# Convolution slots issued in pairs, eight PSUM banks by table, and x1 kept for two images

## The reference

```python
# layer 0: 32 small models of 16 channels, grouped 3x3 neighbourhood, residual
perception = concat([x] + 8 shifted copies, axis=1)      # 9*512 channels
per_g = perception.reshape(b, 32, 144, h, w)
hdn = relu(einsum('bmchw,mdc->bmdhw', per_g, w1) + b1)   # 64 hidden per model
x = x + einsum('bmdhw,mcd->bmchw', hdn, w2) + b2
# layer 1: non-local attention over the 1024 pixels, 128 inner channels
theta, phi, g = (w @ x + b for each of the three)        # 512 -> 128
attn = softmax(theta^T phi); y = attn g                  # 1024 x 1024
out = batchnorm(w_w @ y + w_b) + x
```

## Time and profile before

| | |
|---|---|
| median of 3 runs | 1491.43 us (1491.01 to 1491.73) |
| profiled execution, its own time | 1491.56 us |
| its span, first to last instruction | 1489.8 us |
| TensorE (PE) busy | 1466.9 us, 98% |
| VectorE (DVE) busy | 832.0 us, 56% |
| ScalarE (ACT) busy | 749.4 us, 50% |
| GpSimd (POOL) busy | 241.8 us, 16% |
| DMA | 144 GB/s over the span, 41.4% of 16 engines |
| granted TensorE clock, mean | 1.000 |

### The profile page before, as it was taken

How to read it: one execution, slowest core, us unless ns; L and a number is a source line. 1 busy time by engine, 2 the same in 40 slices (tenths; PEclk the granted TensorE clock), 3 DMA queues, 4 the chain that set the end, 5 groups by cost and what they waited for, 6 DMA issues and landing times.

```text
span 1489.8 us, 27659 instructions
## 1 busy us (share of the span) xinstructions
PE 1466.9 (98%) x10364; PEld 772.7 (52%) x10364; DVE 832.0 (56%) x1033; ACT 749.4 (50%) x1175; POOL 241.8 (16%) x134
## 2 busy tenths in 40 slices
PE   7999999999999999999999999999999999999998
PEld 1454636446464464644546455463644636446467
DVE  1374654746546564565646547465474654656456
ACT  3464463645545454455544646446363554645444
POOL 0040210403103030130401204021040210303003
PEclk9999999999999999999999999999999999999999
DMA  4153452535425263261633625346253452535301
GB/s 134 48 185 117 167 202 90 197 113 173 170 90 208 102 209 135 104 232 67 214 127 128 225 81 196 113 160 211 90 196 114 164 179 90 199 110 200 144 29 57
DMA packets 129280, 214.84 MB, mean 144 GB/s; under 512 B 7280, under 2 KB 78448, under 8 KB 129264
## 3 DMA queue, kind: packets, MB, share of 16 engines
q1 hardware_dynamic: 129264, 214.62, 41.4%
HBM read 110.25 MB, written 104.33 MB: 144 GB/s over the span
## 4 chain that ended last, share of the span: by engine, by line
PE 87%; DVE 4%; issue 3%; DMA 3%; ACT 2%; SPq 0%; ACTq 0%
PE ps L400 27%; PE ps L427 8%; PE ps L414 8%; PE ps L441 6%; PE ps L442 6%; PE ps L443 6%; PE ps L471 4%; PE ps L473 4%; PE ps L472 4%; DMA rows_out<-probs 3%; PE ps L487 3%; DVE neg_max L838 2%; PE ps L457 2%; PE ps L459 2%; PE ps L458 2%
## 5 line engine op out<-in xcount | busy, mean ns | idle before, releaser
L400 PE MATMUL ps<-windows,w_main 64*64 64x512 f32 x4096 | 476.1, 598 | 12.1 <-DMA w_left<-in_w_lefts 9.3
L657 ACT ACTIVATE hidden<-ps,columns 128x512 f32<-128x512 f32 x512 | 310.1, 690 | 265.9 <-PE ps L414 265.9
L1042 POOL TENSOR_TENSOR probs<-probs,row_inv 128x1024 f32<-128x1024 f32 x128 | 241.1, 1893 | 1231.7 <-DVE row_inv L844 1231.7
L400 PEld LDWEIGHTS ps<-windows,w_main 64*64 64x64 f32 x4096 | 142.1, 132 | 303.3 <-issue 302.3
L858 DVE TENSOR_TENSOR x_lo<-x_lo,x_hi 128x1024 fp32r<-128x1024 f32 x120 | 153.7, 1301 | 108.2 <-ACT x_hi L692 107.1
L685 ACT ACTIVATE probs<-ps,neg_max 128x1024 f32<-128x1024 f32 x128 | 143.9, 1124 | 126.4 <-DVE neg_max L838 123.4
L838 DVE TENSOR_REDUCE neg_max<-ps 128x1 f32<-128x1024 f32 x128 | 155.7, 1217 | 14.3 <-PE ps L459 10.6
L441 PE MATMUL ps<-x_hi,wp_hi 128*128 128x512 f32 x384 | 153.5, 400 | 0.6 <-issue 0.6
L442 PE MATMUL ps<-x_lo,wp_hi 128*128 128x512 f32 x384 | 150.0, 391 | 0.0
L443 PE MATMUL ps<-x_hi,wp_lo 128*128 128x512 f32 x384 | 149.6, 390 | 0.0
L849 DVE STREAM_TRANSPOSE probs<-probs 128x1024 f32<-128x1024 f32 x120 | 144.6, 1224 | 0.0
(11 more groups left out here) (78 smaller groups left out, 1511.7 us busy)
## 6 DMA issues: line engine op xcount, KB each, us to landing
rows_out<-probs SPq DMA_DIRECT2D x120, 512.0 KB, 2.8
x_lo<-rows_out SPq DMA_DIRECT2D x120, 512.0 KB, 5.5
out<-out_half SPq DMA_DIRECT2D x30, 1024.0 KB, 4.2
windows<-in_x SPq DMA_DIRECT2D x64, 298.0 KB, 4.1
windows<-in_x SPq DMA_DIRECT2D x64, 264.0 KB, 5.3
rows_out<-g_t SPq DMA_DIRECT2D x15, 512.0 KB, 2.6
g_raw<-rows_out SPq DMA_DIRECT2D x15, 512.0 KB, 7.3
out<-x SPq DMA_DIRECT2D x8, 256.0 KB, 2.1
```

The costliest lines, as they stand in the source:

```text
L400: product = mm(ps[HIDDEN * which:HIDDEN * (which + 1), hidden_bank(n, s, q), :], w_main[rows, p, which, :], shifted(windows[rows, chunk % ...
L657: activation(hidden[:, s % HIDDEN_HELD, q, :], ps[:, hidden_bank(n, s, q), :], ACT.Relu, bias=b1s[:, column:column + 1]).then_inc(hidden_r ...
L1042: nc.gpsimd.tensor_tensor(rows, rows, row_inv[:, e].to_broadcast([P, PIXELS]), ALU.mult).then_inc(normalized, 1)
```

## The change

It leaves the arithmetic and the number of matmuls as they are. `batch(n)` issues two slots in a row (both `mains`, then both `left`), then one piece of attention, then both `dx`; the eight banks are given out by tables; x1 has a buffer for each of two images, and `out` is added in place there, so that `out_half` goes. `hidden` is held for two slots. Because a buffer is now chosen by the parity of n, the loop body is two images and runs 7 turns, with the first image's batch in front of it. The wait at the end of TensorE's body (`out_added`) and that of VectorE's (`stored`) go. `w_left` is loaded in four pieces. All of the engines' orders change, also in the epilogue.

```diff
-HIDDEN_HELD = 4
+HIDDEN_HELD = 2
-        x1 = sb("x1", [P, BLOCKS, PIXELS])
+        x1s = sb("x1s", [P, 2, BLOCKS, PIXELS])
-        out_half = sb("out_half", [P, BLOCKS, HALF])
+        SLOT_BANKS = [(6, 7, 4, 5), (0, 1, 2, 3), (4, 5, 0, 1), (2, 3, 6, 7),
+                      (2, 3, 6, 7), (1, 4, 5, 0), (5, 0, 2, 3), (6, 7, 1, 4)]
+        FIRST_IMAGE_BANKS = [(4, 5, 6, 7), (0, 1, 2, 3)]
+        DX_BANKS = [6, 7, 5, 0, 1, 4, 0, 2]
+        ROW_BANKS = [0, 2, 0, 2, 6, 4, 0, 2]
+        Y_BANKS = [4, 5]
+        Z_BANKS = [(2, 3, 6, 7), (3, 6, 7, 1)]
...
+                elif s == 1:
+                    await_exp(n - 1, 2 + q // 2)
+                elif s == 2:
+                    await_exp(n - 1, 5 + q // 2)
...
+                elif s == 5 and q == 1:
+                    await_ahead(y_split, (n - 1) * 2 + 1)
...
             def scores(n, i):
+                if i >= HALF_QBLOCKS and not last_image(n):
+                    pe.wait_ge(hidden_ready, (n + 1) * SLOT_PAIRS + 2 * (i - HALF_QBLOCKS + 1))
...
             def batch(n, parity):          # TensorE, the order after
                 project(n, 0, TH)
                 project(n, 0, PH)
                 project(n, 1, PH)
                 project(n, 0, G)
                 scores(n, 0)
                 scores(n, 1)
                 project(n, 1, TH)
                 scores(n, 2)
                 project(n, 1, G)
                 scores(n, 3)
                 mains(n + 1, 0)
                 mains(n + 1, 1)
                 left(n + 1, 0)
                 left(n + 1, 1)
                 for i in range(HALF_QBLOCKS, QBLOCKS):
                     scores(n, i)
                 dx(n + 1, 0)
                 dx(n + 1, 1)
                 mains(n + 1, 2)
                 mains(n + 1, 3)
                 left(n + 1, 2)
                 left(n + 1, 3)
                 attend(n, 0)
                 dx(n + 1, 2)
                 dx(n + 1, 3)
                 mains(n + 1, 4)
                 mains(n + 1, 5)
                 left(n + 1, 4)
                 left(n + 1, 5)
                 output(n, 0)
                 dx(n + 1, 4)
                 dx(n + 1, 5)
                 mains(n + 1, 6)
                 mains(n + 1, 7)
                 left(n + 1, 6)
                 left(n + 1, 7)
                 attend(n, 1)
                 dx(n + 1, 6)
                 dx(n + 1, 7)
                 output(n, 1)
-            with pe.Fori(0, BATCH - 1) as n:
-                batch(n)
+            batch(0, 0)
+            with pe.Fori(0, BATCH // 2 - 1) as i:
+                batch(i * 2 + 1, 1)
+                batch(i * 2 + 2, 0)
```

More of the change, by code:

```diff
@@ L184, in conv_attention @@
         w_main_loaded = [sem(f"w_main_loaded_{g}") for g in range(GROUPS)]
-        w_left_loaded = sem("w_left_loaded")
+        w_left_loaded = [sem(f"w_left_loaded_{g}") for g in range(GROUPS)]
         w2_loaded = sem("w2_loaded")
@@ L315, in batch @@
                 fetch_row(n, 7)
[L316 to L317 removed]
+                store_half(n, parity, 0)
+                store_half(n, parity, 1)
             def load_w_main(grp):
@@ L325, in _ @@
                 load_top(0, b)
-            sp.dma_start(w_left[:, :, :, :], w_lefts).then_inc(w_left_loaded, 16)
+            load_w_left(0)
             sp.dma_start(columns[:, :], per_channel).then_inc(columns_loaded, 16)
[L328 to L331, removed]
+            for grp in range(1, GROUPS):
+                load_w_main(grp)
+                load_w_left(grp)
+                if grp == 1:
+                    sp.dma_start(w2s[:, :, :], w2_pairs).then_inc(w2_loaded, 16)
             for b in range(BLOCKS):
@@ L409, in left @@
                 half, grp = divmod(s, GROUPS)
+                if first_image(n) and half == 0:
+                    await_ahead(w_left_loaded[grp], 16)
                 for q in range(GROUP_PAIRS):
@@ L455, in scores @@
                 for half in range(2):
-                    bank, cols = ps[:, 2 * (i % 2) + half, :], slice(half * HALF, (half + 1) * HALF)
+                    bank, cols = ps[:, score_bank(n, i) + half, :], slice(half * HALF, (half + 1) * HALF)
                     mm(bank, tp_hi[:, TH, rows], tp_hi[:, PH, cols], start=True, stop=False)
@@ L475, in attend, with output @@
                 last.then_inc(y_summed, 1)
-            def output(n, h, k):
-                if k == 0:
+            def output(n, h):
+                pe.wait_ge(y_rounded, n * 2 + h + 1)
+                for k in range(BLOCKS):
                     if h == 0:
[L480 to L491, removed]
@@ L493, in batch @@
-            def batch(n):
+                        pe.wait_ge(hidden_ready, (n + 1) * SLOT_PAIRS + 4 * GROUP_PAIRS + k + 1)
+                    bank, c = ps[:, Z_BANKS[h][k], :], slice(k * P, (k + 1) * P)
+                    mm(bank, ww_hi[:, c], y_hi[:, :], start=True, stop=False)
+                    mm(bank, ww_lo[:, c], y_hi[:, :], start=False, stop=False)
+                    if k == 0:
+                        pe.wait_ge(y_split, n * 2 + h + 1)
+                    mm(bank, ww_hi[:, c], y_lo[:, :], start=False, stop=True).then_inc(z_summed, 1)
@@ L506, in batch @@
                 mains(n + 1, 0)
-                scores(n, 4)
-                scores(n, 5)
+                mains(n + 1, 1)
                 left(n + 1, 0)
-                scores(n, 6)
-                scores(n, 7)
-                mains(n + 1, 1)
                 left(n + 1, 1)
-                mains(n + 1, 2)
-                left(n + 1, 2)
+                for i in range(HALF_QBLOCKS, QBLOCKS):
+                    scores(n, i)
                 dx(n + 1, 0)
                 dx(n + 1, 1)
+                mains(n + 1, 2)
@@ L518, in batch @@
                 mains(n + 1, 3)
+                left(n + 1, 2)
                 left(n + 1, 3)
                 attend(n, 0)
[L521 to L528, removed]
                 dx(n + 1, 2)
                 dx(n + 1, 3)
-                mains(n + 1, 6)
-                attend(n, 1)
@@ L533, in batch @@
-                left(n + 1, 6)
-                output(n, 1, 0)
-                output(n, 1, 1)
+                mains(n + 1, 4)
+                mains(n + 1, 5)
+                left(n + 1, 4)
+                left(n + 1, 5)
+                output(n, 0)
                 dx(n + 1, 4)
                 dx(n + 1, 5)
-                output(n, 1, 2)
-                output(n, 1, 3)
+                mains(n + 1, 6)
                 mains(n + 1, 7)
+                left(n + 1, 6)
                 left(n + 1, 7)
-                pe.wait_ge(out_added, n * SLOTS + SLOTS)
+                attend(n, 1)
@@ L545, in transpose_ww @@
+                dx(n + 1, 6)
+                dx(n + 1, 7)
+                output(n, 1)
             def transpose_ww():
@@ L768, in _ @@
             nc.scalar.preload_act_table(ACT.Exp)
-            relus(0, 0)
-            for s in range(1, SLOTS - 1):
+            for s in range(SLOTS):
                 relus(0, s)
-                round_x1(0, s - 1)
-                if s == SLOTS - 3:
+                if 2 <= s < 2 + GROUPS:
+                    round_x1(0, 0, s - 2)
+                if s == SLOTS - 2:
                     act.wait_ge(w_l1_loaded, 16 * W_L1_DMAS)
@@ L947, in batch @@
                 split_row(n, 7)
-                sum_x1(n + 1, 2)
                 split_y(n, 1)
-                sum_x1(n + 1, 3)
-                for k in range(BLOCKS):
-                    add_out(n, 1, k)
-                sum_x1(n + 1, 4)
-                for s in range(GROUPS):
-                    split_x1(n + 1, s)
-                sum_x1(n + 1, 5)
-                split_x1(n + 1, 4)
-                split_x1(n + 1, 5)
-                dve.wait_ge(stored, (n + 1) * 32)
+                split_x1(n + 1, 1 - parity, 0)
+                split_x1(n + 1, 1 - parity, 1)
+                split_x1(n + 1, 1 - parity, 2)
+                split_x1(n + 1, 1 - parity, 3)
+                add_out(n, parity, 1, 0)
+                sum_x1(n + 1, 1 - parity, 6)
+                add_out(n, parity, 1, 1)
+                add_out(n, parity, 1, 2)
+                add_out(n, parity, 1, 3)
+                sum_x1(n + 1, 1 - parity, 7)
             steps = [0]
@@ L981, in _ @@
             chain(tt(shift[:, :], shift[:, :], bn[:, BETA, :], ALU.add))
-            for s in range(SLOTS - 2):
-                sum_x1(0, s)
-                split_x1(0, s)
-                if s == SLOTS - 4:
+            for s in range(SLOTS):
+                sum_x1(0, 0, s)
+                if 2 <= s < 2 + GROUPS:
+                    split_x1(0, 0, s - 2)
+                if s == SLOTS - 2:
                     dve.wait_ge(w_l1_loaded, 16 * W_L1_DMAS)
```

361 lines of the change are left out of this document (198 added, 163 removed).

## The result

The changed kernel takes 1479.37 us (1478.04 to 1480.44, 4 runs) against 1491.58 us for the kernel before on the same chip: a ratio of 0.9918, 95% interval 0.9901 to 0.9935, so faster, by 12.2 us. The forecast was 1469 us in a range of 1457 to 1484: the direction and the range held, the gain was a little over half of the one forecast. The profiled execution took 1478.04 us with a span of 1476.2.

The account below looks back on a forecast made before the run. TensorE's own stream bounds the kernel, busy 90.90 of 91.14 us per turn. Span: 1489.8 - 28.3 (loop) + 0.3 (prologue) + 0.1 (epilogue) + 6 (code fetches) = 1467.9 us; forecast 1469 us, range 1457 to 1484.

Parts of the forecast that it names:

- Fewer changes of shape: TensorE's stream: 17 stretches of one shape per turn instead of 30, saving 2.2 us of 91.14.
- The waits of the old order go: TensorE's waits for the exponential and the late bank of the sixth mains vanish, 0.5 us per turn.
- The x1 chain: VectorE's splits and sums ahead of project(n, 1, PH): 10.3 us against 10.2, a wait of about 0.1 us, no reserve.
- Scores 4 and the relus: scores(4) writes banks that relus 0 and 1 read, so TensorE waits 0.5 us behind the two left.
- Turned rows: Row 3's split ends about 1 us ahead of the first attend, row 7 has 3 us; cost 0, at most 1.
- The longer body: The doubled loop body may not fit on chip; fetches at six jumps back cost 1 us each, 6 us.
- Prologue +0.3, epilogue +0.1: Code outside the loop: prologue gains and losses sum to +0.3 us, epilogue's to +0.1, give or take 3.
- The softmax: Exponentials of rows 3 and 6 finish shortly before mains(1) and mains(2) want their banks; taken as 0, at most 0.5 each.
- `dx` 5: TensorE's dx 5 waits 0.15 us for its relus.
- waits take the gain back: Rival: small-reserve handovers cost the gain, giving no change at 1490 or 1491 + 6, or likelier halfway, 1480; chance 0.14.
- Code loading: Rival: the jump back finds no block and following blocks come late, 11 us at each jump, 1529 us; chance 0.07.

Follow-up runs that it names:

- e6: e3 with the other three pairs of slots taken apart (mains, left, mains, left), the first pair kept; 1480.85 us.
- e5: e3 with TensorE's first pair of slots taken apart (mains 0, left 0, mains 1, left 1); 1462.92 us.
- e3: The changed kernel with VectorE's invert_sum 5 and 6 moved behind the three split_row, so GpSimd normalizes rows 5 and 6 after them; 1467.09 us.
- e4: The changed kernel with all loops of 7 turns written out, so that no engine jumps back; 1472.83 us.
- e2: The kernel before with only the loop changed: first batch in front, then 7 turns of two images each; 1521.37 us.
- e7: e3 with the kernel before's orders in the last image from the third score on, including turn_row(7) ahead of attend_turned(2); 1465.52 us.
- e10: The changed kernel with only TensorE's loop boundary moved by 24 products, to behind project(n + 1, 0, PH); 1474.95 us.
- e1: The changed kernel with GpSimd's normalize cut from 1024 to 32 columns of each row block, all semaphores kept; 1467.06 us.

## Why the prediction was right, and where its size was off

- *Fewer changes of shape, 2.2 us per turn*: right. A pair saves 0.35 (e6), so four save 1.4 where I had 0.5 + 0.6. TensorE's busy time fell by 2.4; less this and the 0.2 of the late sixth `mains`, 0.8 is left for the merged 128x128 stretches, where I had 1.1. No experiment takes these apart alone.
- *The waits of the old order go, 0.5 us*: right.
- *The x1 chain, 0.1 us at the third projection*: right. The four projections take 11.01 us from 691.60, behind a jump, and 11.10 from 781.34: there the third starts 0.32 us behind the product before it, where 0.23 is usual.
- *Scores 4 and the relus, 0.5 us*: right, it costs 0.62, and e5 shows the mechanism.
- *Turned rows, cost 0, at most 1 us*: this is the step that failed. I had the end of the splits 1 us ahead of `attend`, and left GpSimd out of the reckoning. `split_g` and three `split_row` take 7.4 us together instead of 4.7, since GpSimd's `normalize` of rows 5 and 6 runs among them, and `attend` waits 0.77 in each turn. That is 11.5 us (e3: 12.3), more than the whole miss of 10.4. The kernel before had the sign of it: 15 of its 120 `split_row`, one in each turn, take up to 1.85 us where the median is 1.23; the one at 553.49 ends 1.1 us behind GpSimd's end at 554.23. The Trainium skill, "SBUF — State Buffer", section SBUF: two separate sides, states it: a VectorE instruction with two SBUF inputs contends with a GpSimd instruction that reads SBUF, and the pair of ports is a lock held for the whole instruction. The trace agrees to 0.1 us (the 1.1 us behind 733.97).
- *The longer body, 6 x 1 us*: right in size (e4: 6.5), for a reason that I had only half. A fetch is not 2.8 us but, as an estimate, about 4 (the gap of 0.92 us and the 12 products, 2.85 us, that ran on ahead of it); e2 shows 2.6 to 4.7 us of idle time with little handed over. It was mostly hidden because the change also set 12 output products ahead of the jump. Whether taking away the wait at the end of the body helped was not measured by itself. In the kernel before, with its old end of the body, a jump costs 5 us (e2), partly through the clock, which the prediction did not have. The Trainium skill, "Runtime: NRT & Kernel Launch", Instruction fetch mechanics, was right that such a body does not stay: 100 packets against 12.
- *Prologue +0.3, epilogue +0.1*: -0.3 and +0.5. The first projection starts at 59.9 instead of 60.2, and from the last image's at 1413.2 it takes 63.0 us instead of 62.5. `turn_row(7)` waits 2.45 us where I had 2.3; the 1.3 us of slow clock that can follow (e7) was not foreseen.
- *The softmax, 0 us, and `dx` 5, 0.15 us*: right; no wait for the softmax is in the list, and `dx` 5 waits 0.2 us.

Of the rivals, "waits take the gain back" came halfway, at 1480, as priced, but not as it was made up: it had 1.2 us at the x1 chain, which came to 0.1, and 0.3 at the turned rows, which came to 0.77. Code loading did not decide here; 5 us at each of six jumps, as in e2, would have taken more than the gain. The executions of the changed kernel spread over 2.4 us, where the kernel before spreads over 0.8. The clock goes with it: the mean granted clock was 1.000 in the shortest, which is the profiled one, 0.999 in the two of 1479.3 and 1479.4, and 0.998 in the one of 1480.44. With what the traces of e3, e4 and e10 show behind the wait of L619, that is the likely cause; the longer executions of the changed kernel itself were not profiled.

## What to carry to other kernels

When an engine's order is rewritten, place GpSimd's instructions too: two engines with slack in the totals can block each other exactly where the critical engine will wait, and moving the tiny instruction that releases the one is the cheapest cure. When a loop body grows past what the engine holds, put the jump where the most work is already handed over, or write the loop out. Grouping work of one shape pays on TensorE, but group only as far as the engine behind it can take its results at once.

## What the runs showed of the hardware

- A change of tile shape costs TensorE about 0.16 us behind a stretch of 64x64 tiles, 0.19 behind one of 32x64 (e6) and 0.22 around one of 128x128 products.
- A body of 1282 matmuls and loads is held (12 blocks for the whole run), one of twice that is fetched again in each turn (100 blocks). With one `left` as the last work ahead of it, the jump leaves TensorE idle for 2.6 to 4.7 us; behind the first, of 4.34 us, it works for 3.0 us at the 1.2 GHz level (e2).
- An idle time of 2.45 us in the last image is followed by such a slow stretch in the traces of e1, e3, e4, e6 and e10, and by none in those of the changed kernel and e5. It costs 1.3 us in e4.
- A VectorE subtraction of two SBUF operands waits for a running GpSimd multiplication to end and the reverse: three such subtractions, 3.49 us in e3, took 5.17 beside one multiplication, and that one took 2.80 instead of 1.89.
